# Splitting the row maxima of the windowed attention into two operations of two heads, each with its own signal

## The chip, the core and the metric

The kernel runs on one core of a Trainium2 chip, in one launch. The time is the device time of one execution in microseconds (us). Five engines work side by side and are tied together by semaphores only: TensorE (PE; its weight loads are listed as PEld), VectorE (DVE), ScalarE (ACT), GpSimd (POOL) and SyncE (SP), which issues the DMAs.

## What is computed

The reference adds four layers to `x` (16 sequences of 512 tokens, 128 features): an attention with a Gaussian kernel, a feed-forward layer, a state-space layer, and the same feed-forward layer again. The feed-forward layer has a light branch (windowed attention over all tokens) and a heavy branch (attention over routed tokens). The change is in the light branch:

```
x: (16, 512, 128); H = 8 heads of 64; windows of W = 64 tokens
q, k, v = split(layernorm(x) @ Wqkv.T, 3)
sim  = q_window . k_(previous, own, next window) / 8        # 64 x 192 for a window and head
attn = softmax(sim, axis=-1)                                # max, exp, sum, divide
o    = attn . v_(previous, own, next window)
light = o @ Wout.T
route: 50 rounds of a = logk - logsumexp(s + b), b = -relu(s + a)
```

## The kernel before, in words

The program runs `stage_rbf`, then a light stage and a heavy stage (names with `f1`), the state-space stage, and a second light and heavy stage (`f2`). The change touches `stage_light` alone, which runs twice (f1 from about 465 to 980 us, f2 from about 1206 to 1714 us).

In a light stage a **unit** is a block of 128 tokens (two windows) with four of the eight heads (`HU` = 4). A sequence has 8 units, the stage 128. A **step** t does the two units of one block of 128 tokens; there are 64 steps, four to a sequence (i = t mod 4). For a unit n the engines do this in turn:

- TensorE, `scores(n)` (L917, L903): q times k for four heads, 192 columns a head, into `sm`, which has two PSUM banks for each unit, two heads in each.
- VectorE, `maxima(n)` (L1221): one reduction of 128x768 to the 4 negated maxima `nb`.
- ScalarE, `exps(n)` (L1103): for each head exp(score - maximum) into `p`, with the row sum, which appears in the trace as an ACTIVATE and an ACTIVATION_READ_ACCUMULATOR.
- VectorE, `reciprocals(n)` (L1228); GpSimd, `normalise(n)` (L1534): `p` times the reciprocal, into `pn`.
- TensorE, `turn(n)` (L933 for the first 512 columns into `tp`, L941 for the others): transposes.
- VectorE, `leave_turned(n)` (L1234, L1236): copies them to `pt`.
- TensorE, `values(n)` (L964, L975): times v, into `xa`; ScalarE, `leave_late(n)` (L1095): copies half of it to `late`; VectorE, `leave_values(n)` (L1244): adds both halves into `ot`; TensorE, `output` (L989): times the output weights.

The order on each engine is written by hand in its function `step(t)`. Work of several steps is interleaved; the next sequence's projections go along (`use` on TensorE, L869 to L879, three a step; `leave` on ScalarE, L1077 to L1081), and so do the routing rounds (`route`, `route_shift`, `route_step`):

- TensorE: turn(2t), output, turn(2t+1), three projections, values(2t), scores(2t+4), scores(2t+5), values(2t+1). The second projection goes to `tp` and waits until the copy L1234 of unit 2t+1 has emptied it; turn(2t+1) waits for the copy L1234 of unit 2t for the same reason.
- VectorE: maxima(2t+2), maxima(2t+3), copies of unit 2t, reciprocals(2t+2), copies of unit 2t+1, residual, leave_values(2t-1), route_shift, reciprocals(2t+3), leave_values(2t).
- ScalarE: exps(2t+2) head 0, leave_late(2t-1), exps(2t+2) heads 1 to 3, exps(2t+3) heads 0 to 2, leave, exps(2t+3) head 3, leave, leave, leave_late(2t), route.

Of the kernel before, what the change touches and what calls it, by code (L numbers as in the profile page):

```python
# [10 lines left out]
ALU = mybir.AluOpType  # L11
ACT = mybir.ActivationFunctionType
AX = mybir.AxisListType.X
# [72 lines left out]
def wait(e, sem, v):  # L86

    if isinstance(v, int) and v <= 0:
        return
    e.wait_ge(sem, v)  # L90
# [601 lines left out]
def stage_light(nc, K, tag, C=None):  # L692
# [13 lines left out]
    with ExitStack() as ctx:  # L706
# [3 lines left out]
        PW = P + W  # L710
# [7 lines left out]
        nb = sb("nb", [P, 2, HU])  # L718
        sums = sb("sums", [P, 2, HU])
        rs = sb("rs", [P, 2, HU])  # L720
        p = sb("p", [P, 2, HU, PW])
# [6 lines left out]
        sm = ps("sm", [P, 2, 2, BANK])  # L728
# [17 lines left out]
        s_nb = sem("nb")  # L746
        s_ex = sem("ex")
        s_rs = sem("rs")
        s_nm = sem("nm")
# [51 lines left out]
        def place(n):  # L801

            return n // UNITS, n // UNITS % 2, n % UNITS
# [266 lines left out]
        def _(act):  # L1070
# [25 lines left out]

            def exps(n, heads):
                u = n % UNITS
                if heads[0] == 0:
                    act.wait_ge(s_nb, n + 1)  # L1100
                    wait(act, s_nm, n - 1)
                for k in heads:
                    ins = nc.scalar.activation(p[:, u % 2, k, :], sm[:, u % 2, k // 2, k % 2 * PW:(k % 2 + 1) * PW],  # L1103
                                               ACT.Exp, bias=nb[:, u % 2, k:k + 1], accum_out=sums[:, u % 2, k:k + 1])
                if heads[-1] == HU - 1:
                    ins.then_inc(s_ex, 1)
# [48 lines left out]
            if C:  # L1155
                leave_rows(0)
                leave_rows(1)
                for b in range(2, B):
                    if b < 6:
                        exps(b // 4, (b % 2 * 2, b % 2 * 2 + 1))  # L1160
                    leave_rows(b)
                    if b - 2 in WITH:
                        leave(0, WITH[b - 2])
                leave_x(1)
            else:
                exps(0, (0, 1, 2, 3))
                leave(0, 9)
                leave(0, 10)
                exps(1, (0, 1, 2, 3))
                leave(0, 11)  # L1170
                leave(0, 12)
                leave_x(1)
# [43 lines left out]
        def _(dve):  # L1216
            def maxima(n):
                b, par, u = place(n)
                dve.wait_ge(s_sm, n + 1)
                wait(dve, s_ex, n - 1)  # L1220
                nc.vector.tensor_reduce(nb[:, u % 2, :], sm[:, u % 2, :, 0:2 * PW].rearrange("p a (k c) -> p a k c", k=2),  # L1221
                                        AX, ALU.max, negate=True).then_inc(s_nb, 1)

            def reciprocals(n):
                b, par, u = place(n)
# [183 lines left out]
            if C:  # L1409
# [13 lines left out]
                for b in range(4, 9):  # L1423
                    rows(b)
                maxima(0)
                maxima(1)
                rows(9)
                rows(10)
# [7 lines left out]
                link(nc.vector.reciprocal(two[:, 1, :], two[:, 1, :]))  # L1436
                link(nc.vector.tensor_scalar(K["rc"][:], two[:, 1, :], float(np.sqrt(np.float32(E))), None, ALU.mult))
                maxima(2)
                maxima(3)
            else:  # L1440
# [1014 lines left out]
```

## Time and profile before

| | |
|---|---|
| median of 3 runs | 1840.35 us (1833.6, 1840.35, 1841.53) |
| profiled execution | 1834.43 us, span of its trace 1832.6 us |
| granted TensorE clock, mean of the span | 0.975 |
| PE busy | 1660.2 us (91%) |
| DVE busy | 1449.5 us (79%) |
| ACT busy | 1451.2 us (79%) |
| POOL busy | 748.7 us (41%) |

The profile is of one execution. Times are microseconds from the start of the span. A row of a timeline has the start, the duration, the engine, the line, the operation, what it writes and reads, and its shape; x2 means that two alike were merged, and the duration then runs from the start of the first to the end of the second. A bracket at the end is idle time of the engine just before, and what ended it. Short waits have no bracket. The ends of matmuls are modelled.

### The profile page before, as it was taken

What the parts mean: (1) busy time and instruction counts of PE and PEld (TensorE: products, weight loads), DVE (VectorE), ACT (ScalarE), POOL (GpSimd) and SP (SyncE); (2) the same over time, 40 slices, a digit from 0 to 9 for tenths busy, and PEclk for the clock granted to TensorE, in tenths of its full rate; (3) what the DMA queues carried; (4) which work ended last, traced back from release to release, by engine and by line L of the source; (5) the groups of instructions that cost most, each with busy time, mean ns of one, the idle gap of its engine ahead of it and who ended that gap; (6) DMA issues with size and microseconds to landing.
All of it is one profiled execution on the core that took longest, in us unless ns stands there. A gap on an engine that the chain in (4) does not pass through costs nothing. (4 is left out here: it accounts for less than half of the span.)

```text
span 1832.6 us, 68018 instructions
## 1 busy us (share of the span) xinstructions
PE 1660.2 (91%) x27513; PEld 1268.5 (69%) x27513; DVE 1449.5 (79%) x3461; ACT 1451.2 (79%) x4100; POOL 748.7 (41%) x842
## 2 busy tenths in 40 slices
PE   3888898886899999999997987879999999998797
PEld 1444444443688888888885874658888888887686
DVE  8999999998677777877896766747777777788574
ACT  4999999996788888888774656668888888876464
POOL 2010000000254555454545866435555555454595
PEclk7999999999999999999999997989999999999999
DMA  6555656561001010101012000001010101000211
GB/s 190 147 154 151 150 125 149 137 148 27 13 15 26 14 26 14 26 15 25 15 26 48 2 2 1 1 13 25 15 26 14 26 15 24 15 17 23 48 47 48
DMA packets 80040, 91.95 MB, mean 50 GB/s; under 512 B 11696, under 2 KB 67984, under 8 KB 79728
## 3 DMA queue, kind: packets, MB, share of 16 engines
q1 hardware_dynamic: 78432, 87.15, 19.0%
q8 instruction: 220, 3.60, 0.8%
q14 instruction: 92, 0.75, 0.1%
q10 hardware_dynamic: 1296, 0.44, 0.1%
HBM read 39.68 MB, written 31.10 MB: 39 GB/s over the span
## 5 line engine op out<-in xcount | busy, mean ns | idle before, releaser
L1534 POOL TENSOR_TENSOR f1l_pn<-f1l_p,f1l_rs 128x512 f32<-128x512 f32 (+1 forms) x256 | 206.3, 827 | 245.0 <-DVE f1l_rs L1228 240.0
L1534 POOL TENSOR_TENSOR f2l_pn<-f2l_p,f2l_rs 128x512 f32<-128x512 f32 (+1 forms) x256 | 206.2, 827 | 236.6 <-DVE f2l_rs L1228 236.6
L1103 ACT ACTIVATE f2l_p<-f2l_sm,f2l_nb 128x192 f32<-128x192 f32 x512 | 209.1, 434 | 41.7 <-DVE f2l_nb L1221 41.7
L1103 ACT ACTIVATE f1l_p<-f1l_sm,f1l_nb 128x192 f32<-128x192 f32 x512 | 209.3, 434 | 40.6 <-DVE f1l_nb L1221 37.3
L417 PE MATMUL r_acc<-r_pr,r_vp 128*32 128x128 f32 (+2 forms) x3584 | 191.4, 330 | 7.1 <-DVE r_pr L630 6.0
L527 ACT ACTIVATE r_pr<-r_far 128x1536 f32<-128x1536 f32 x128 | 194.3, 1518 | 3.3 <-PE r_far L401 3.0
L622 DVE SCALAR_TENSOR_TENSOR r_pr<-r_pr,k_lo,r_cap 128x512 f32<-128x512 f32 x256 | 181.1, 750 | 6.3 <-ACT r_pr L527 5.7
L630 DVE TENSOR_SCALAR r_pr<-r_pr,k_hi,k_lo 128x768 f32<-128x768 f32 x256 | 163.7, 683 | 0.0
L527 ACT ACTIVATE r_pr<-r_near 128x1024 f32<-128x1024 f32 x128 | 138.6, 1083 | 1.1 <-PE r_near L388 1.1
L1539 POOL MEMSET k_rtz<- 128x132 f32 x1 | 0.2, 207 | 329.4 <-POOLq L688 329.4
L1221 DVE TENSOR_REDUCE f2l_nb<-f2l_sm 128x4 f32<-128x768 f32 x128 | 116.2, 949 | 16.5 <-PE f2l_sm L917 16.5
L1221 DVE TENSOR_REDUCE f1l_nb<-f1l_sm 128x4 f32<-128x768 f32 x128 | 116.2, 949 | 13.4 <-PE f1l_sm L917 13.4
L417 PEld LDWEIGHTS r_acc<-r_pr,r_vp 128*32 128x32 f32 x3584 | 87.1, 110 | 46.8 <-issue 28.2
L1244 DVE TENSOR_TENSOR f2l_ot<-f2l_xa,f2l_late 128x256 f32<-128x256 f32 x128 | 53.9, 421 | 78.2 <-ACT f2l_late L1095 78.2
L1103 ACT ACTIVATION_READ_ACCUMULATOR f2l_p<-f2l_sm,f2l_nb 128x1 f32 x512 | 112.7, 220 | 0.0
L1103 ACT ACTIVATION_READ_ACCUMULATOR f1l_p<-f1l_sm,f1l_nb 128x1 f32 x512 | 112.5, 220 | 0.0
L1234 DVE COPY f1l_pt<-f1l_tp 128x512 f32<-128x512 f32 x128 | 88.1, 689 | 28.3 <-PE f1l_tp L933 25.1
L1234 DVE COPY f2l_pt<-f2l_tp 128x512 f32<-128x512 f32 x128 | 88.2, 689 | 23.4 <-PE f2l_tp L933 20.8
L1244 DVE TENSOR_TENSOR f1l_ot<-f1l_xa,f1l_late 128x256 f32<-128x256 f32 x128 | 53.9, 421 | 63.0 <-ACT f1l_late L1095 62.8
L917 PE MATMUL f2l_sm<-f2l_kt,f2l_qt 64*64 64x128 f32 (+1 forms) x3584 | 99.3, 248 | 0.4 <-ACT f2l_p L1103 0.4
L917 PE MATMUL f1l_sm<-f1l_kt,f1l_qt 64*64 64x128 f32 (+1 forms) x3584 | 99.1, 248 | 0.0
L964 PE MATMUL f1l_xa<-f1l_pt,f1l_vv 64*64 64x128 f32 x2048 | 85.1, 276 | 12.0 <-DVE k_x L1250 7.0
(525 smaller groups left out, 5090.5 us busy)
## 6 DMA issues: line engine op xcount, KB each, us to landing
rbf_rows<-r_part SPq DMA_DIRECT2D x112, 128.0 KB, 2.2
r_qs<-rbf_rows SPq DMA_DIRECT2D x60, 192.0 KB
r_ks<-rbf_rows SPq DMA_DIRECT2D x60, 192.0 KB
f1l_vs<-f1l_vv SPq DMA_DIRECT2D x64, 128.0 KB, 2.6
f2l_vs<-f2l_vv SPq DMA_DIRECT2D x64, 128.0 KB, 2.4
rbf_rows<-r_part SPq DMA_DIRECT2D x16, 384.0 KB, 3.2
rbf_rows<-r_part SPq DMA_DIRECT2D x16, 256.0 KB, 3.2
out<-k_x SPq DMA_DIRECT2D x8, 512.0 KB, 3.2
```

Of the source, the lines that this page charges most:

```text
L417: mm = nc.tensor.matmul(acc[32 * g:32 * g + 32, q0:q0 + n], vp[:, par, t, g, 32 * q:32 * q + 32], pr[:, (PAIRS * b + 2 * q + g // 2) % RIN ...
L527: nc.scalar.activation(pr[:, n % RING, :, cols], src, ACT.Exp).then_inc(done, 1)
L622: nc.vector.scalar_tensor_tensor(on, on, K["lo"][:, h:h + 1], cap[:, h, :].unsqueeze(1).broadcast_to([P, NT, P]), ALU.max, ALU.min)
L630: ins = nc.vector.tensor_scalar(off, off, hi, lo, ALU.min, ALU.max)
L917: mm = nc.tensor.matmul(sm[64 * w:64 * w + 64, u % 2, e, cc * PW + P * side:cc * PW + P * side + kn], qt[r, par, c, at:at + W], kt[r, par, ...
L964: nc.tensor.matmul(xa[64 * e:64 * e + 64, r, cc * P:(cc + 1) * P], vv[rows, par, i, cc, g, e, :], pt[rows, u % 2, k * P:(k + 1) * P], star ...
L1103: ins = nc.scalar.activation(p[:, u % 2, k, :], sm[:, u % 2, k // 2, k % 2 * PW:(k % 2 + 1) * PW], ACT.Exp, bias=nb[:, u % 2, k:k + 1], ac ...
L1221: nc.vector.tensor_reduce(nb[:, u % 2, :], sm[:, u % 2, :, 0:2 * PW].rearrange("p a (k c) -> p a k c", k=2), AX, ALU.max, negate=True).the ...
L1234: nc.vector.tensor_copy(pt[:, u % 2, 0:HU * P], tp[:]).then_inc(s_pt, 1)
L1244: nc.vector.tensor_tensor(ot[:, u // 2 % 2, 2 * g:2 * g + 2, :], xa[:, 0, 0:2 * P].rearrange("p (c q) -> p c q", q=P), late[:, u % 2, :].r ...
L1534: ins = nc.gpsimd.tensor_tensor(pn[:, u % 2, at:at + HU * w].rearrange("p (k c) -> p k c", k=HU), p[:, u % 2, :, cols], r.broadcast_to([P, ...
L1539: nc.gpsimd.memset(K["rtz"][:], 0.0).then_inc(s_rt, 1)
```

## The change

`maxima` issues two reductions instead of one, for heads 0 and 1 and for heads 2 and 3 (the two PSUM banks of a unit), and each raises the semaphore `s_nb` by one. `exps` waits before head 0 and again before head 2, each time for the reduction that covers the head.

```diff
             def exps(n, heads):
                 u = n % UNITS
-                if heads[0] == 0:
-                    act.wait_ge(s_nb, n + 1)
-                    wait(act, s_nm, n - 1)
                 for k in heads:
+                    if k % 2 == 0:
+                        act.wait_ge(s_nb, 2 * n + k // 2 + 1)
+                    if k == 0:
+                        wait(act, s_nm, n - 1)
...
-                nc.vector.tensor_reduce(nb[:, u % 2, :], sm[:, u % 2, :, 0:2 * PW].rearrange("p a (k c) -> p a k c", k=2),
-                                        AX, ALU.max, negate=True).then_inc(s_nb, 1)
+                for a in range(2):
+                    nc.vector.tensor_reduce(nb[:, u % 2, 2 * a:2 * a + 2],
+                                            sm[:, u % 2, a, 0:2 * PW].rearrange("p (k c) -> p k c", k=2),
+                                            AX, ALU.max, negate=True).then_inc(s_nb, 1)
```

VectorE, at the start of a step in f2's light stage, before (in brackets the semaphores that an instruction waits for: l_sm is signalled by the scores, l_ex by the exps, l_t4 by the transposes L933):

```order
L1244 TENSOR_TENSOR f2l_ot<-f2l_xa,f2l_late 128x256 [waits l_w,l_ov]
L1221 TENSOR_REDUCE f2l_nb<-f2l_sm 128x4 [waits l_ex,l_sm] x2
L1234 COPY f2l_pt<-f2l_tp 128x512 [waits l_t4,l_pv]
L1236 COPY f2l_pt<-f2l_pj 128x256 [waits l_t]
L1261 SCALAR_TENSOR_TENSOR k_na<-k_lns,k_m,k_router_rows 128x1 [waits l_sl]
```

The same place now (lines after the change are 3 higher):

```order
L1247 TENSOR_TENSOR f2l_ot<-f2l_xa,f2l_late 128x256 [waits l_w,l_ov]
L1223 TENSOR_REDUCE f2l_nb<-f2l_sm 128x2 [waits l_ex,l_sm]
L1223 TENSOR_REDUCE f2l_nb<-f2l_sm 128x2
L1223 TENSOR_REDUCE f2l_nb<-f2l_sm 128x2 [waits l_ex,l_sm]
L1223 TENSOR_REDUCE f2l_nb<-f2l_sm 128x2
L1237 COPY f2l_pt<-f2l_tp 128x512 [waits l_t4,l_pv]
```

Two reductions have become four; nothing else has moved. ScalarE, from the end of one step into the next, before (l_nb is the maxima's signal, l_nm GpSimd's, l_pv that of the values, l_pp that of a projection):

```order
L1131 ACTIVATE k_lns<-k_sum 128x1 [waits l_sl]
L1103 ACTIVATE f2l_p,f2l_sums<-f2l_sm,f2l_nb 128x192 [waits l_nm,l_nb]
L1095 ACTIVATE f2l_late<-f2l_xa 128x256 [waits l_oe,l_pv]
L1103 ACTIVATE f2l_p,f2l_sums<-f2l_sm,f2l_nb 128x192 x3
L1103 ACTIVATE f2l_p,f2l_sums<-f2l_sm,f2l_nb 128x192 [waits l_nm,l_nb]
```

The same place now:

```order
L1132 ACTIVATE k_lns<-k_sum 128x1 [waits l_sl]
L1104 ACTIVATE f2l_p,f2l_sums<-f2l_sm,f2l_nb 128x192 [waits l_nm,l_nb]
L1095 ACTIVATE f2l_late<-f2l_xa 128x256 [waits l_oe,l_pv]
L1104 ACTIVATE f2l_p,f2l_sums<-f2l_sm,f2l_nb 128x192
L1104 ACTIVATE f2l_p,f2l_sums<-f2l_sm,f2l_nb 128x192 [waits l_nb]
L1104 ACTIVATE f2l_p,f2l_sums<-f2l_sm,f2l_nb 128x192
L1104 ACTIVATE f2l_p,f2l_sums<-f2l_sm,f2l_nb 128x192 [waits l_nm,l_nb]
```

The order is the same; each unit's third head has a wait that it had not.

## Rows read from the trace of the kernel before

**Rows 1.** Busy time of each engine in the two light stages.
```profile
core 0: us, PE busy (x) PEld busy (x) DVE busy (x) ACT busy (x) POOL busy (x), PEclk, DMA share, GB/s
465.00:980.00 515.00, 498.44 (x9364) 421.39 (x9362) 403.07 (x1054) 425.85 (x1526) 254.01 (x306) 1.00 0.08 19
1206.00:1714.00 508.00, 491.85 (x9344) 420.50 (x9344) 378.29 (x909) 416.54 (x1508) 254.08 (x306) 1.00 0.08 19
```
**Rows 2.** The instructions and waits around the tile nb, f1's and f2's.
```profile
L1221 DVE TENSOR_REDUCE f1l_nb<-f1l_sm x128: 947/948/958, 470.1 to 968.4; 128x4 f32<-128x768 f32 x128
  ACT f1l_p L1103: 37.3, 58
...
L1221 DVE TENSOR_REDUCE f2l_nb<-f2l_sm x128: 947/948/959, 1214.6 to 1696.0; 128x4 f32<-128x768 f32 x128
...
  ACT f2l_p L1103: 41.7, 63
```
**Rows 3.** Timeline of VectorE, from a step with i = 1 into that with i = 3.
```profile
1380.01 1.81 DVE L1221 TENSOR_REDUCE f2l_nb<-f2l_sm 128x4 f32<-128x768 f32 x2
1381.77 0.69 DVE L1234 COPY f2l_pt<-f2l_tp 128x512 f32<-128x512 f32 x1
...
1383.35 0.69 DVE L1234 COPY f2l_pt<-f2l_tp 128x512 f32<-128x512 f32 x1 [0.15 <-PE f2l_tp L933]
...
1387.06 0.42 DVE L1244 TENSOR_TENSOR f2l_ot<-f2l_xa,f2l_late 128x256 f32<-128x256 f32 x1 [1.43 <-ACT f2l_late L1095]
1387.40 1.81 DVE L1221 TENSOR_REDUCE f2l_nb<-f2l_sm 128x4 f32<-128x768 f32 x2
1389.32 0.69 DVE L1234 COPY f2l_pt<-f2l_tp 128x512 f32<-128x512 f32 x1
...
1395.63 1.82 DVE L1221 TENSOR_REDUCE f2l_nb<-f2l_sm 128x4 f32<-128x768 f32 x2 [0.60 <-PE f2l_sm L917]
1397.61 0.69 DVE L1234 COPY f2l_pt<-f2l_tp 128x512 f32<-128x512 f32 x1 [0.16 <-PE f2l_tp L933]
```
**Rows 4.** Timeline of TensorE over the same time.
```profile
1380.85 0.23 PE L975 MATMUL f2l_xa<-f2l_pt,f2l_vs 64*64 64x64 f32 x2
1381.01 0.66 PE L933 MATMUL f2l_tp<-k_ident,f2l_pn 128*128 128x128 f32 x4
...
1382.61 0.63 PE L933 MATMUL f2l_tp<-k_ident,f2l_pn 128*128 128x128 f32 x4
...
1384.09 0.50 PE L869 MATMUL f2l_tp<-f_xh,k_wqkv_l 128*128 128x512 f32 x1
...
1385.68 0.67 PE L964 MATMUL f2l_xa<-f2l_pt,f2l_vv 64*64 64x128 f32 x16
...
1388.56 0.66 PE L933 MATMUL f2l_tp<-k_ident,f2l_pn 128*128 128x128 f32 x4
...
1390.16 0.62 PE L933 MATMUL f2l_tp<-k_ident,f2l_pn 128*128 128x128 f32 x4
...
1396.84 0.66 PE L933 MATMUL f2l_tp<-k_ident,f2l_pn 128*128 128x128 f32 x4
```
**Rows 5.** Timeline of ScalarE, the step with i = 1.
```profile
1380.28 0.20 ACT L1131 ACTIVATE k_lns<-k_sum 128x1 f32<-128x1 f32 x1
1380.99 0.42 ACT L1103 ACTIVATE f2l_p<-f2l_sm,f2l_nb 128x192 f32<-128x192 f32 x1 [0.51 <-DVE f2l_nb L1221]
...
1381.40 0.37 ACT L1095 ACTIVATE f2l_late<-f2l_xa 128x256 f32<-128x256 f32 x1
...
1385.79 0.60 ACT L1079 ACTIVATE f2l_kt<-f2l_pj 128x512 f32<-128x512 f32 x1
1386.65 0.38 ACT L1095 ACTIVATE f2l_late<-f2l_xa 128x256 f32<-128x256 f32 x1 [0.26 <-PE f2l_xa L975]
```
**Rows 6.** Reductions of another width, in the heavy stage (by line and shape; mean in ns).
```profile
L1927 DVE TENSOR_REDUCE f2h_nb<-f2h_ps 128x4 f32<-128x516 f32 x16 | 10.4, 690 | 19.6 <-PE f2h_ps L1725 19.6
```
**Rows 7.** Timeline of VectorE at the start of f2's light stage.
```profile
1217.32 0.18 DVE L1228 RECIPROCAL f2l_rs<-f2l_sums 128x4 f32<-128x4 f32 x1 [0.92 <-ACT f2l_p L1103]
1219.90 0.18 DVE L1228 RECIPROCAL f2l_rs<-f2l_sums 128x4 f32<-128x4 f32 x1 [2.40 <-ACT f2l_p L1103]
```

## The prediction

> **What bounds the kernel now.** I read the busy times by stage first [rows 1]. In both light stages TensorE is busy for 97% of the time at the full granted clock, VectorE for 74 to 78%, ScalarE for 82 to 83%, GpSimd for half. No engine is plainly full but TensorE, whose ends are modelled, so the limit has to be read from the waits. Next the tile that the change splits: ScalarE waited 37.3 us in 58 waits (f1) and 41.7 us in 63 waits (f2) for the maxima [rows 2]. That is 79 us of waiting, and the question is whether any of it is on the path. So third, the timelines of one sequence's steps, where the period of a step is 7.39 us (1380.01 to 1387.40) or 8.23 us (1387.40 to 1395.63) [rows 3].
>
> Followed back, the loop is this. VectorE copies the transposed unit 2t out of `tp` (starts 1381.77, ends 1382.46) [rows 3]; TensorE's next transposes start at 1382.61, a hand-over later, and end at 1383.24 [rows 4]; VectorE copies again at 1383.35 with a wait marked for just these [rows 3], ending at 1384.04; TensorE's second projection, which needs that bank, starts at 1384.09, the values at 1385.68 [rows 4]; ScalarE takes them out at 1386.65, having idled 0.26 us for TensorE [rows 5]; VectorE adds them at 1387.06, having idled 1.43 us, and then comes to the next two maxima at 1387.40 [rows 3]. The maxima stand on this loop where the copy behind them is late because of them. The exps do not: between the first exp and the late copy at 1386.65 ScalarE twice had to wait for TensorE's products anyway.
>
> **Is the copy behind the maxima late because of them?** Two readings of the same instant. By TensorE: the transposes of unit 2t end at 1381.67 and the copy starts at 1381.77, 0.10 later; the transposes that end at 1383.24 are followed by a copy at 1383.35, 0.11 later and marked as a wait [rows 3, 4]. So the copy started when TensorE let it. By VectorE: two reductions take 1.81 us together and one takes 0.948 [rows 2, 3], so the second starts 0.86 after the first and 0.09 before the record of the first ends; the copy could thus have started at 1380.01 + 1.81 - 0.08 = 1381.74. VectorE was ready 0.03 us before TensorE. This is the tight kind of step, i = 0 and 1. In the step with i = 2 VectorE was ready at 1387.40 + 1.73 = 1389.13 and the copy started at 1389.32 (transposes end 1389.22): 0.19 us of slack. With i = 3, 1395.63 + 1.74 = 1397.37 against 1397.61: 0.24 us [rows 3, 4]. These are the loose kind. The four steps repeat in the other sequences of both stages.
>
> **The change part by part.**
>
> *One more reduction for each unit, 256 in all.* A reduction of 768 elements takes 0.948 us [rows 2], one of 516 takes 0.690 [rows 6]: 1.02 ns an element. One of 384 comes to 0.948 - 0.39 = 0.56 us. From start to start it takes 0.08 to 0.09 less, as the pairs show, so about 0.47, and the two halves 0.94 instead of 0.86 to 0.87: 0.07 us more for each unit, 0.14 for each step. The bounds: at least 0.06 (what is left if the element takes a little more), and at most the whole fixed part of a record, 0.948 - 768 x 0.00102 = 0.16 us, if two halves do not overlap as two wholes do. I take 0.07, because the pairs of [rows 3] already have a signal and a wait between them and overlap all the same.
>
> *In a tight step* 0.14 us, less 0.03 of slack, goes on the loop: 0.11. There are 64 such steps in two stages; the first of each stage, and the ones where TensorE is late by more (around the start and the end of the routing search), do not count, so I take 60: 60 x 0.11 = 6.6 us.
>
> *In a loose step* 0.14 us disappears under the 0.19 or 0.24 us that the copy waits for TensorE. Cost 0. That cover is gone above 0.19.
>
> *ScalarE's first exp starts earlier.* It started at 1380.99, 0.03 us behind the first reduction's end (1380.96), after 0.51 us of idling [rows 3, 5]. With half the reduction it can start 0.39 us earlier. But the next instruction there is the late copy of unit 2t-1, which needs the values whose matmuls end at 1381.08 [rows 4] and started at 1381.40 [rows 5] only because the exp was in front of it; it can move up 0.26 at most with its hand-over. So the exps behind it gain some 0.26 us. What waits for them: the reciprocals, which are ahead of GpSimd's work, which has a whole step to spare; the late copy of unit 2t, which waits for TensorE already (0.26 idle). Worth 0 on the loop. What is late next is TensorE, as before.
>
> *The added wait, before head 2.* Its signal comes 0.47 us after the first one's, while head 0, the late copy and head 1 take over 0.9 us of ScalarE. So it is never waited for; the wait itself is issued on an engine with slack ahead of the late copy. Cost 0, at worst a few hundredths that the 0.26 covers.
>
> *The start of a stage* is a plain chain: there VectorE waited 0.92 and 2.40 us for the exps [rows 7], and the first maxima are in front of them. Up to 0.39 us is gained in each stage: -0.8 us.
>
> *Sum:* 6.6 - 0.8 = +5.8 us on the profiled execution's 1834.43, that is 1840.2. The median shown is 5.9 us above that execution; what I compare with is the median, so 1840.35 + 5.8 = 1846 us.
>
> The Trainium skill, in "VectorE: DVE Perf Modes", section "The DRAIN you can't avoid", says that the next operation does not start before the pipeline has emptied; its section on the errata puts the fixed term of an operation at about 150 cycles, 0.156 us, and its rules for authors say to minimise the count of operations. The trace shows the overlap of 0.09 us between two reductions, so I read the price of one more as 0.07; by the page's term it would be an estimate of 0.156, which is the first rival's price.
>
> **The rivals.**
>
> *1. The full fixed part is paid.* If each half costs 0.16 us more, a step costs 0.32. Tight steps: 0.29 x 60 = 17 us; loose steps: 0.13 and 0.08, 30 of each: 6 us. With the starts, +22.6, so 1863 us. For it: no row shows two reductions of the same unit without a wait between, nor one of 384 elements. Against: every pair of rows of VectorE that stands back to back overlaps.
>
> *2. ScalarE sets the end (faster).* If the loop is really closed by ScalarE, from first exp to late copy, then every one of the 121 waits [rows 2] shortens by 0.26 us (the late copy of unit 2t-1 holds the rest back): -31 us, 1809. For it: the 79 us of waits, and only 0.26 us of idling ahead of the late copy. It decides as soon as that 0.26 is not a true wait. Against: the bracket names TensorE's L975 as what ended it [rows 5], and in the same step VectorE and TensorE hand over to each other without a gap.
>
> *3. Nothing is on the path.* If the slack of a tight step is more than the 0.03 read, say TensorE's transposes have 0.1 to give before the next transposes are late, the reductions cost nothing anywhere and the two starts gain: 1839 to 1841 us. For it: TensorE is 97% busy and may itself be the limit. Against: the second transposes start 0.15 behind the end of the copy in the tight step (1382.46, 1382.61) and in the loose one (1390.01, 1390.16) [rows 3, 4]; a queue of TensorE's own would not keep that distance when the copy moves.
>
> **How the numbers follow.** My forecast (+3 to +9 us) has 0.55, rival 1 (or a price between) 0.17, rival 2 or a part of it 0.12, rival 3 0.16. About 0.5%, 9.2 us, is what a measurement can tell from no change. Faster by more than that is rival 2 alone: 0.12. Slower by more is rival 1 and the upper end of my own: 0.23. The rest, 0.65, is the same. The forecast's own range is 1843 to 1850; for 8 in 10 it reaches up to rival 1's time and down past rival 3 some way into the partial gains: 1830 to 1863.
>
> **What would show it.** Right: reductions of about 0.56 us, four of them in 1.88 to 1.96 us from the first start to the last end; the copy L1234 behind them 1.87 us after the first start in tight steps (before 1.76), its distance to the transposes larger than 0.10 there and unchanged in loose ones; a tight step's period up by 0.1, the loose ones' unchanged; ScalarE's wait ahead of the first exp down from 0.51 to about 0.1, and a new wait ahead of the late copy that follows it. Wrong: tight periods that are unchanged (rival 3), loose periods longer (rival 1), or the late copy of unit 2t earlier relative to the maxima in every step (rival 2).

## The result and the profile after

The changed kernel takes 1842.33 us (median of 20 runs, 1836.08 to 1848.83), the kernel before 1839.61 us in the runs beside it (20 runs, 1833.6 to 1844.07). The ratio is 1.0023, with an interval of 1.0013 to 1.0033: 4.2 us slower, 2.4 to 6.1 (the two medians alone differ by 2.7 us, the two means by 3.8). That is a real difference, and within 0.5%. The profiled execution took 1842.14 us, its span is 1840.4 us, the granted clock 0.971 over the span (0.975 before). In the bulk of both light stages (500 to 960 us and 1240 to 1690 us) the clock is 1.00 in both traces, so what the steps there take is compared at one clock. VectorE has 256 instructions more and is busy for 1458.6 us instead of 1449.5.

The reductions first, by tile, with those who waited for them (min/median/max in ns, first and last start; this answers to [rows 2]):

```profile
L1223 DVE TENSOR_REDUCE f1l_nb<-f1l_sm x256: 543/547/558, 471.8 to 972.4; 128x2 f32<-128x384 f32 x128
...
  ACT f1l_p L1104: 14.7, 13
```
```profile
L1223 DVE TENSOR_REDUCE f2l_nb<-f2l_sm x256: 543/547/558, 1219.9 to 1704.0; 128x2 f32<-128x384 f32 x128
...
  ACT f2l_p L1104: 14.8, 15
```

A half takes 0.547 us, and ScalarE's listed waits for the maxima have fallen from 79.0 us in 121 waits to 29.5 us in 28, while the kernel became slower. The list overstates what went. It leaves out short waits, and the usual wait is now such a short one, of 0.11 us; counted in full from the traces, ScalarE's idling ahead of a unit's first exp falls from 82.3 to 37.3 us. Most of that went elsewhere: all idle time of ScalarE in the two light stages, every gap counted, is 171.0 us now and was 176.6.

VectorE in three steps, of the kinds that [rows 3] shows: 1378.08 and 1385.45 begin tight steps, 1392.94 and 1401.16 loose ones.

```profile
1378.08 1.94 DVE L1223 TENSOR_REDUCE f2l_nb<-f2l_sm 128x2 f32<-128x384 f32 x4
1379.94 0.68 DVE L1237 COPY f2l_pt<-f2l_tp 128x512 f32<-128x512 f32 x1
...
1385.45 1.94 DVE L1223 TENSOR_REDUCE f2l_nb<-f2l_sm 128x2 f32<-128x384 f32 x4
1387.31 0.68 DVE L1237 COPY f2l_pt<-f2l_tp 128x512 f32<-128x512 f32 x1
1388.87 0.69 DVE L1237 COPY f2l_pt<-f2l_tp 128x512 f32<-128x512 f32 x1 [0.34 <-PE f2l_tp L933]
1392.60 0.42 DVE L1247 TENSOR_TENSOR f2l_ot<-f2l_xa,f2l_late 128x256 f32<-128x256 f32 x1 [1.44 <-ACT f2l_late L1095]
1392.94 1.94 DVE L1223 TENSOR_REDUCE f2l_nb<-f2l_sm 128x2 f32<-128x384 f32 x4
1394.86 0.69 DVE L1237 COPY f2l_pt<-f2l_tp 128x512 f32<-128x512 f32 x1
...
1401.16 1.95 DVE L1223 TENSOR_REDUCE f2l_nb<-f2l_sm 128x2 f32<-128x384 f32 x4 [0.59 <-PE f2l_sm L917]
1403.14 0.69 DVE L1237 COPY f2l_pt<-f2l_tp 128x512 f32<-128x512 f32 x1
```

Four halves take 1.94 us from first start to last end, where two wholes took 1.81. In a tight step the copy starts 1.86 us behind the first of them (1385.45 to 1387.31); before it was 1.76 (1380.01 to 1381.77 in [rows 3]). In a loose step it is 1.92 and 1.98, as before. The medians over the steps of each kind say the same. They are given for i = 0, 1, 2, 3, worked out from the starts in the two traces; the period is that from one step's first maxima to the next step's:

| from the first maxima of a step to | before | after |
|---|---|---|
| the copy behind them | 1.76, 1.76, 1.92, 1.98 | 1.86, 1.86, 1.92, 1.98 |
| the first exp | 0.98, 0.98, 0.98, 0.99 | 0.58, 0.58, 0.58, 0.65 |
| the late copy of unit 2t-1 | 1.39, 1.39, 1.39, 1.40 | 1.14, 1.14, 1.28, 1.34 |
| the late copy of unit 2t (f1) | 6.52, 6.63, 6.79, 6.74 | 6.61, 6.73, 6.79, 6.73 |
| period (f1) | 7.28, 7.39, 8.23, 7.49 | 7.37, 7.49, 8.23, 7.49 |
| all four steps of a sequence, the sum of these | 30.39 | 30.57 |

The row on the late copy of unit 2t tells how far ScalarE's head start reaches: it has the first exp 0.40 us earlier and, in tight steps, the first late copy 0.26 earlier, but the late copy at the end of the step, which the loop goes through, is 0.09 to 0.10 later where the copy was delayed and unchanged elsewhere. ScalarE in the step that begins at 1385.45 shows where the gained time went (compare [rows 5]):

```profile
1385.72 0.20 ACT L1132 ACTIVATE k_lns<-k_sum 128x1 f32<-128x1 f32 x1
1386.03 0.42 ACT L1104 ACTIVATE f2l_p<-f2l_sm,f2l_nb 128x192 f32<-128x192 f32 x1
...
1386.59 0.39 ACT L1095 ACTIVATE f2l_late<-f2l_xa 128x256 f32<-128x256 f32 x1
...
1389.71 0.60 ACT L1079 ACTIVATE f2l_kt<-f2l_xa 128x512 f32<-128x512 f32 x1 [0.33 <-PE f2l_xa L873]
...
1392.18 0.38 ACT L1095 ACTIVATE f2l_late<-f2l_xa 128x256 f32<-128x256 f32 x1 [0.26 <-PE f2l_xa L975]
```

The 0.51 us of idling ahead of the first exp is down to 0.11 (1385.92 to 1386.03). The late copy that follows starts 0.56 us behind the exp instead of 0.41: a short new wait for the values. Six exps later ScalarE comes 0.33 us too early for a projection, and ahead of the late copy of unit 2t it idles 0.26 us, just as before.

The stages, from the first maxima to the last `ot`, are 516.84 and 499.51 us long, against 513.59 and 497.07: +3.3 and +2.4. That is 5.7 of the 7.8 us between the two spans; the other 2 us lie outside the light stages, where nothing was changed. The runs of either kernel lie 10 to 13 us apart, so 2 us between two executions need no cause of their own.

### The profile page after: what moved, and what is told of

Read it like the earlier page. It is cut to its first block and busy times, and to the rows that moved or that the text cites. A ratio compares the mean times of both kernels' runs of the same rounds, so it can differ in the third digit from the quotient of the medians.

```text
span 1840.4 us, 68274 instructions
## 1 busy us (share of the span) xinstructions
PE 1669.7 (91%) x27513; PEld 1273.7 (69%) x27513; DVE 1458.6 (79%) x3717; ACT 1463.2 (80%) x4100; POOL 749.3 (41%) x842
## 5 line engine op out<-in xcount | busy, mean ns | idle before, releaser
L1104 ACT ACTIVATE f2l_p<-f2l_sm,f2l_nb 128x192 f32<-128x192 f32 x512 | 209.0, 430 | 18.8 <-DVE f2l_nb L1223 14.8
L1223 DVE TENSOR_REDUCE f2l_nb<-f2l_sm 128x2 f32<-128x384 f32 x256 | 124.3, 547 | 16.2 <-PE f2l_sm L917 16.2
L1223 DVE TENSOR_REDUCE f1l_nb<-f1l_sm 128x2 f32<-128x384 f32 x256 | 124.4, 547 | 13.6 <-PE f1l_sm L917 13.6
L1237 DVE COPY f1l_pt<-f1l_tp 128x512 f32<-128x512 f32 x128 | 87.7, 685 | 27.7 <-PE f1l_tp L933 27.3
L1237 DVE COPY f2l_pt<-f2l_tp 128x512 f32<-128x512 f32 x128 | 87.7, 685 | 23.3 <-PE f2l_tp L933 22.4
```

The lines of the kernel that those rows point to most:

```text
L1223: nc.vector.tensor_reduce(nb[:, u % 2, 2 * a:2 * a + 2], sm[:, u % 2, a, 0:2 * PW].rearrange("p (k c) -> p k c", k=2), AX, ALU.max, negate ...
L1237: nc.vector.tensor_copy(pt[:, u % 2, 0:HU * P], tp[:]).then_inc(s_pt, 1)
```

## The experiments

Each was timed side by side with the kernel before, in 4 to 12 executions, and the ratios are to that kernel. The edits of 1 to 4, 7 and 9 are shown against the changed kernel, those of 5, 6 and 8 against the kernel before. L numbers are those of each kernel's own lines. "A sequence takes" stands for the sum of the four periods, as in the table above; in f1 and f2 of one trace it agrees within 0.03 us.

**1. Two reductions, but ScalarE waits for both.** It separates the cost on VectorE from the gain on ScalarE.

```diff
-                    if k % 2 == 0:
-                        act.wait_ge(s_nb, 2 * n + k // 2 + 1)
                     if k == 0:
+                        act.wait_ge(s_nb, 2 * n + 2)
```

> The two reductions of each unit stay, but ScalarE waits for both of them before head 0, as before the change. Theory (the cost is VectorE's added time on the loop through the copies, and ScalarE's earlier start buys nothing but the start of each stage): the same time as the changed kernel within 1.5 us, ratio to before 1.002 to 1.004; tight steps at 7.36 and 7.48 us as in the changed kernel. Rival (the early start was worth something all along and paid a part of a larger cost): slower than the changed kernel by what it was worth, up to 0.26 us in each of some 120 steps, 31 us; ratio above 1.006.

Measured: 1843.75 us, ratio 1.0025 (1.0013 to 1.0037). ScalarE waits again, more than before the change:

```profile
L1222 DVE TENSOR_REDUCE f2l_nb<-f2l_sm x256: 544/548/559, 1220.6 to 1706.3; 128x2 f32<-128x384 f32 x128
...
  ACT f2l_p L1103: 46.3, 63
```

14.8 us of waits have become 46.3 (41.7 before the change), and the four steps of a sequence take the same 30.57 us as with the early start. In steady state the second signal is worth nothing. The light stages are 0.85 and 1.4 us longer than in the changed kernel. Only part of this lies at a start: in f2 the first copy L1237 (here L1236) starts 7.74 us behind the stage's first maxima, against 7.29 in the changed kernel, and in f1 there is no difference. The rest comes in a few jumps of 0.3 to 1.1 us at single steps later in the stages; such jumps also lie between the other traces, and their cause was not looked for.

**2 and 3. The halves in loose steps only, and in tight steps only.** The same edit with opposite sets, (2, 3) in experiment 2 and (0, 1) in 3; the counts of the semaphore follow it.

```diff
+        def halved(n):
+            return (n // 2 - 1) % NT in (2, 3)
+
+        def signals(n):
+            return sum(1 + halved(m) for m in range(n))
...
+                    if k == 0 or (k == 2 and halved(n)):
+                        act.wait_ge(s_nb, signals(n) + k // 2 + 1)
...
+                if halved(n):
...
+                else:
+                    nc.vector.tensor_reduce(nb[:, u % 2, :],
...
```

> Units whose maxima are taken in steps with i = 2 or 3 are halved, the others have one reduction as before the change. Theory: the copy behind them waits 0.19 to 0.24 us for TensorE there, which covers 0.13 us: ratio to before 0.999 to 1.001, periods of all four steps as before (7.27, 7.39, 8.22, 7.49). Rival (each added reduction costs its time wherever it stands): half of the change's cost, +2 to +3 us, ratio 1.001 to 1.0015, with the periods behind i = 2 and 3 longer by 0.1.

> Units whose maxima are taken in steps with i = 0 or 1 are halved, the others have one reduction. Theory: the whole cost of the change, +4 to +6 us, ratio 1.002 to 1.003, tight periods longer by 0.09, the others as before. Rival (cost wherever it stands): half of it, ratio 1.001 to 1.0015.

Measured: loose only 1837.53 us, ratio 0.9995 (0.998 to 1.0009); tight only 1842.71 us, ratio 1.0022 (1.0009 to 1.0035). So the 64 tight steps, of 128 in the two stages, carry the loss: with them alone it is there, with the loose ones alone none is measured. VectorE with halves in loose steps (first a tight step, then a loose one):

```profile
1377.91 1.81 DVE L1234 TENSOR_REDUCE f2l_nb<-f2l_sm 128x4 f32<-128x768 f32 x2
1379.67 0.69 DVE L1248 COPY f2l_pt<-f2l_tp 128x512 f32<-128x512 f32 x1
...
1393.86 1.95 DVE L1230 TENSOR_REDUCE f2l_nb<-f2l_sm 128x2 f32<-128x384 f32 x4 [0.59 <-PE f2l_sm L923]
1395.84 0.69 DVE L1248 COPY f2l_pt<-f2l_tp 128x512 f32<-128x512 f32 x1
```

And with halves in tight steps:

```profile
1379.80 1.94 DVE L1230 TENSOR_REDUCE f2l_nb<-f2l_sm 128x2 f32<-128x384 f32 x4
1381.66 0.68 DVE L1248 COPY f2l_pt<-f2l_tp 128x512 f32<-128x512 f32 x1
...
1403.23 1.82 DVE L1234 TENSOR_REDUCE f2l_nb<-f2l_sm 128x4 f32<-128x768 f32 x2 [0.60 <-PE f2l_sm L923]
1405.21 0.69 DVE L1248 COPY f2l_pt<-f2l_tp 128x512 f32<-128x512 f32 x1 [0.16 <-PE f2l_tp L939]
```

The distance from maxima to copy is 1.76 (tight, whole), 1.98 (loose, halved), 1.86 (tight, halved) and 1.98 (loose, whole). A loose step has the same length with either, apart from the bracket: with halves VectorE's idling ahead of the copy, 0.16 us for TensorE, is nearly used up. A sequence takes 30.40 us with halves in loose steps and 30.57 with halves in tight ones.

**4. Four reductions for each unit, one for each head.** This goes past the slack of every step.

```diff
-                for a in range(2):
-                    nc.vector.tensor_reduce(nb[:, u % 2, 2 * a:2 * a + 2],
...
+                for k in range(HU):
+                    nc.vector.tensor_reduce(nb[:, u % 2, k:k + 1], sm[:, u % 2, k // 2, k % 2 * PW:(k % 2 + 1) * PW],
+                                            AX, ALU.max, negate=True).then_inc(s_nb, 1)
...
+                    if k % 2 == 0:
-                        act.wait_ge(s_nb, 2 * n + k // 2 + 1)
+                        act.wait_ge(s_nb, 4 * n + k + 2)
```

> Four reductions for each unit, of one head each; ScalarE waits for two of them before head 0 and for all before head 2. A step has 6 more reductions than before the change, at 0.065 us from start to start: +0.39 us on VectorE. Theory (VectorE's time counts above each step's slack of 0.03, 0.03, 0.19 and 0.24 us): 0.36 in 60 tight steps, 0.20 and 0.15 in 30 loose steps each, 21.6 + 6 + 4.5 = 32 us less about 0.5 at the starts; ratio 1.015 to 1.019. Rival (proportional to the number of reductions, 4.2 us for two more in each step): 12.6 us, ratio 1.007. Rival (the cost lies in signals and waits, not in VectorE's time): ScalarE has no more waits than in the changed kernel, so 1.002 to 1.004.

Measured: 1868.75 us, ratio 1.0155 (1.0131 to 1.0179), some 28 us. The reductions and copies, a tight step and a loose one:

```profile
L1223 DVE TENSOR_REDUCE f2l_nb<-f2l_sm x512: 344/348/359, 1232.9 to 1730.5; 128x1 f32<-128x192 f32 x171
```
```profile
1379.10 2.20 DVE L1223 TENSOR_REDUCE f2l_nb<-f2l_sm 128x1 f32<-128x192 f32 x8
1381.22 0.68 DVE L1236 COPY f2l_pt<-f2l_tp 128x512 f32<-128x512 f32 x1
...
1387.51 2.21 DVE L1223 TENSOR_REDUCE f2l_nb<-f2l_sm 128x1 f32<-128x192 f32 x8 [0.59 <-PE f2l_sm L917]
1389.63 0.68 DVE L1236 COPY f2l_pt<-f2l_tp 128x512 f32<-128x512 f32 x1
```

The copy now starts 2.12 us behind the first maxima in every step, tight or loose (2.13 with i = 3): VectorE sets it everywhere. Six more reductions in a step take 2.20 - 1.81 = 0.39 us more, 0.065 each. A sequence takes 31.40 us, 1.01 more than before. By the copies, unrounded, the tight steps pay 0.35 each and the loose ones 0.20 and 0.15, 1.05 together.

**5. One reduction over two heads, for all four.** It leaves out the maxima of heads 2 and 3: one 128x384 reduction for heads 0 and 1, whose two maxima serve heads 2 and 3 as well.

```diff
-                                               ACT.Exp, bias=nb[:, u % 2, k:k + 1], accum_out=sums[:, u % 2, k:k + 1])
+                                               ACT.Exp, bias=nb[:, u % 2, k % 2:k % 2 + 1], accum_out=sums[:, u % 2, k:k + 1])
...
-                nc.vector.tensor_reduce(nb[:, u % 2, :], sm[:, u % 2, :, 0:2 * PW].rearrange("p a (k c) -> p a k c", k=2),
+                nc.vector.tensor_reduce(nb[:, u % 2, 0:2],
+                                        sm[:, u % 2, 0, 0:2 * PW].rearrange("p (k c) -> p k c", k=2),
```

> One reduction for each unit, over heads 0 and 1 only, and heads 2 and 3 use those two maxima as their own (part of the maxima is left out): VectorE has 0.40 us less for each unit, 0.80 less for each step, and ScalarE can start 0.4 us earlier, more than any split could give. Theory (with the maxima out of the way TensorE's own chain sets the loop): only the slack that VectorE lacked and the starts are gained, 0 to 0.03 us a step; ratio 0.996 to 1.000. Rival (VectorE or ScalarE sets the loop and the change would have paid with a cheaper reduction): 0.26 to 0.8 us a step, 30 to 90 us, ratio 0.95 to 0.985.

Measured: 1836.56 us, ratio 0.9986 (0.9973 to 1.0000). VectorE in a tight step:

```profile
1379.37 1.14 DVE L1221 TENSOR_REDUCE f2l_nb<-f2l_sm 128x2 f32<-128x384 f32 x2
1381.14 0.69 DVE L1235 COPY f2l_pt<-f2l_tp 128x512 f32<-128x512 f32 x1 [0.62 <-PE f2l_tp L933]
```

VectorE is ready 0.67 us sooner (1.14 instead of 1.81) and waits 0.62 us for TensorE's transposes; the copy still starts 1.76 us behind the maxima (median), and a sequence takes 30.41 us. So before the change TensorE, not VectorE, let the copy start, and there is nothing to win on VectorE's side of this place. The 3 us of the median are not in the steps of the trace, and its interval touches 1. The expectation counted on 0.80 us less for VectorE. The missing part is the overlap: these two reductions, of different units, start 0.58 us apart or more in all but three pairs, at least 0.03 behind the end of the record in front, where halves of the same width in the changed kernel start 0.464 apart. Why they don't overlap here stays open.

**6 and 7. The transposes of the next unit ahead of the values.** If TensorE's transposes are what the copy waits for, having them earlier should speed up the kernel and bring the price of the halves back in all steps. On TensorE `turn(2t+2)` moves from the start of a step to ahead of `values(2t+1)` of the step before; experiment 6 does it to the kernel before, 7 to the changed one.

```diff
-                turn(2 * t)
+                if t == 0:
+                    turn(0)
...
+                if t + 1 < T:
+                    turn(2 * t + 2)
                 values(2 * t + 1)
```

> The kernel before, with one move on TensorE: the transposes of unit 2t+2 are issued ahead of the values of unit 2t+1 instead of behind them, so that the copy behind the maxima waits for VectorE alone and starts 1.73 us after the first maxima in every step (1.76, 1.76, 1.92 and 1.98 us before). Theory A (the copy's start is what a step turns on, as in the prediction): the loop is shorter by 0.03, 0.03, 0.19 and 0.25 us, 0.5 a sequence, 15 us in two stages; ratio 0.991 to 0.994. Theory B (TensorE's own work between the two transposes, the values and the output, is only just covered by that copy, and is now moved between them): the second transposes start when they did, the gain is under 0.03 us a step; ratio 0.998 to 1.001.

> The changed kernel with the same move on TensorE. Theory A: the copy starts 1.86 us after the first maxima in every step, against 1.76, 1.76, 1.92 and 1.98 us before: -0.10, -0.10, +0.06, +0.12 us a sequence of gain, so about the time of the kernel before, ratio 0.999 to 1.002. Theory B: the tight steps stay 0.09 us longer than before and the loose ones do not gain: the changed kernel's time, ratio 1.001 to 1.004. In either case the split costs against e6, since with TensorE out of the way VectorE's added 0.13 us stands uncovered in all four steps: by 0.10 to 0.13 us a step, 12 to 16 us, under A, and by 5 to 8 us under B.

Measured: 1881.63 us, ratio 1.0244 (1.0224 to 1.0264), and 1882.8 us, ratio 1.0249 (1.0225 to 1.0273). Both expectations missed by far. ScalarE and VectorE in a tight step of experiment 6:

```profile
1405.94 0.42 ACT L1106 ACTIVATE f2l_p<-f2l_sm,f2l_nb 128x192 f32<-128x192 f32 x1 [0.51 <-DVE f2l_nb L1224]
...
1407.06 0.38 ACT L1098 ACTIVATE f2l_late<-f2l_xa 128x256 f32<-128x256 f32 x1 [0.61 <-PE f2l_xa L975]
```
```profile
1404.96 1.81 DVE L1224 TENSOR_REDUCE f2l_nb<-f2l_sm 128x4 f32<-128x768 f32 x2
1406.69 0.68 DVE L1237 COPY f2l_pt<-f2l_tp 128x512 f32<-128x512 f32 x1
...
1408.68 0.18 DVE L1231 RECIPROCAL f2l_rs<-f2l_sums 128x4 f32<-128x4 f32 x1 [0.86 <-ACT f2l_p L1106]
1408.78 0.67 DVE L1237 COPY f2l_pt<-f2l_tp 128x512 f32<-128x512 f32 x1
```

The copy did start earlier: 1.73 us behind the maxima in every step (1.74 with i = 3), as VectorE alone allows. Against the 1.76, 1.76, 1.92 and 1.98 of before, this measures the slack that the prediction had read: 0.03, 0.03, 0.19 and 0.24 us. But the values behind the transposes are later, and ScalarE's late copy of unit 2t-1 waits for them *in front of* the exps of heads 1 to 3: 2.10 us behind the maxima instead of 1.39. The exps are late, the reciprocals wait for them, and the second copy stands behind the reciprocals on VectorE: 2.09 us after the first (1406.69 to 1408.78) instead of 1.57. A sequence takes 32.22 us. Experiment 7, where the copy stands 1.86 us behind the maxima, takes the same 32.22. The loop had changed its course, so the pair says little on what the earlier transposes are worth.

**8 and 9. The same, with the late copy behind three exps.** To take that block away: on ScalarE `exps(2t+2)` of heads 0 to 2, then `leave_late(2t-1)`, then head 3. Experiment 8 is 6 with this edit, 9 is 7 with it.

```diff
-                    exps(2 * t + 2, (0,))
+                    exps(2 * t + 2, (0, 1, 2))
...
-                    exps(2 * t + 2, (1, 2, 3))
+                    exps(2 * t + 2, (3,))
```

> As e6 (transposes of unit 2t+2 ahead of the values of unit 2t+1), and ScalarE takes the late copy of unit 2t-1 behind heads 0 to 2 of the next unit instead of behind head 0. In e6 that late copy waited 0.6 us for TensorE and held back the exps, so that VectorE's reciprocals (39.9 us in 42 waits) and the copy behind them came late. Theory (that hold-up was all of e6's loss): the reciprocals wait no longer, and the question of e6 can be answered: gain of the copy's start by 0.03, 0.03, 0.19 and 0.25 us passed on (A, ratio 0.991 to 0.994) or kept by TensorE's own work between the two transposes (B, 0.998 to 1.002). Rival (the values behind the transposes make everything after them late as well, the adds and the output): still over 1.015.

> e8 with the maxima in two halves. Under A: slower than e8 by 0.13 us in each step, 12 to 16 us, as nothing covers VectorE's time; under B: slower than e8 by 3 to 8 us. Rival: if exps are what VectorE waits for in e8, the earlier first exp is worth something at last, up to 0.4 us a step, and e9 is faster than e8.

Measured: 1864.79 us, ratio 1.0149 (1.0132 to 1.0167), and 1867.17 us, ratio 1.0164 (1.0147 to 1.0181). The block is gone (VectorE's waits for exps ahead of the reciprocals, from 1250 to 1600 us, are 4.9 us where experiment 6 had 39.9), and 17 us came back. Neither theory that was put down for 8 came true (ratio 0.991 to 0.994, or 0.998 to 1.002); its rival, that the later values make what follows late as well, asked for over 1.015 and is the nearest. For 9 at least 3 us over 8 were expected; the medians differ by 2.4 us, with intervals that overlap. VectorE in experiment 9:

```profile
1403.96 1.94 DVE L1226 TENSOR_REDUCE f2l_nb<-f2l_sm 128x2 f32<-128x384 f32 x4
1405.82 0.68 DVE L1240 COPY f2l_pt<-f2l_tp 128x512 f32<-128x512 f32 x1
1407.63 0.69 DVE L1240 COPY f2l_pt<-f2l_tp 128x512 f32<-128x512 f32 x1 [0.57 <-PE f2l_tp L933]
```

The first copy is 1.86 behind the maxima, as in the changed kernel, but the second waits 0.57 us for TensorE, and a sequence takes 31.70 us with whole reductions and with halves. Here the halves are hidden in every step, tight or not. What keeps these two slow is, by this, TensorE's own sequence. TensorE in experiment 8:

```profile
1403.19 1.52 PE L917 MATMUL f2l_sm<-f2l_kt,f2l_qt 64*64 64x128 f32 x64
1404.64 0.66 PE L933 MATMUL f2l_tp<-k_ident,f2l_pn 128*128 128x128 f32 x4
1405.13 0.38 PE L941 MATMUL f2l_pj<-k_ident,f2l_pn 128*128 128x128 f32 x2
1405.44 0.67 PE L964 MATMUL f2l_xa<-f2l_pt,f2l_vv 64*64 64x128 f32 x16
...
1406.15 1.16 PE L989 MATMUL f2l_xa<-k_wout_l,f2l_ot 128*128 128x128 f32 x8
1407.15 0.60 PE L933 MATMUL f2l_tp<-k_ident,f2l_pn 128*128 128x128 f32 x4
```

and in the kernel before (its rows from the first transposes on are in [rows 4]):

```profile
1379.01 1.52 PE L917 MATMUL f2l_sm<-f2l_kt,f2l_qt 64*64 64x128 f32 x64
1380.35 0.62 PE L964 MATMUL f2l_xa<-f2l_pt,f2l_vv 64*64 64x128 f32 x16
```

From the scores to the second transposes it is 3.96 us (1403.19 to 1407.15) against 3.60 (1379.01 to 1382.61) for the same work, and there the second transposes stand 0.15 us behind the end of a copy that they wait for, so TensorE's own part is 3.60 at most. Four times 0.36 is 1.4 us a sequence, and 1.3 were lost (31.70 against 30.39). The order 64x64 tiles, 128x128, 64x64, 128x128 has two changes more than 64x64, then 128x128. That the changes themselves cost the 0.36 us is read from this order and was not tried alone.

## Why the prediction was right, point by point

1846 us was forecast with an own range of 1843 to 1850 and a wider one of 1830 to 1863; 1842.33 was measured, which is in the wider range and 0.7 us below the own one. The forecast as a difference was +5.8 us (+3 to +9), the measured one +4.2 (2.4 to 6.1). The call "within 0.5%" held. Of the 3.7 us between 1846 and 1842.33, 0.7 are the base: 1840.35 was the median of three runs, 1839.61 that of twenty.

- *What bounds the kernel.* Right. The loop goes over the copy, TensorE and the late copy; giving ScalarE all of its waits for the maxima back cost nothing in steady state (experiment 1), and halving VectorE's maxima left the copy where it was (experiment 5).
- *The price of one more reduction, taken as 0.07 of 0.06 to 0.16.* Measured 0.065, and the same by two halves as by four quarters. The records are 0.948, 0.547 and 0.348 us for 768, 384 and 192 elements, 1.04 ns an element and a fixed part of 0.148; two of them back to back overlap by about 0.083, and the rest is 0.065. The price was the difference of two nearly equal numbers, the fixed part and the overlap, and both could be read from the kernel before.
- *Tight steps, 0.11 each.* Right in kind, a little high: 0.09 to 0.10. The copy came 0.096 later; behind four halves it also takes 0.68 instead of 0.69 us. The price was taken 0.005 too high for each reduction, and the slack of 0.03 was right. By the periods that is 0.18 us a sequence (0.09 and 0.10 in tight steps, nothing in loose ones), and over all 32 sequences of both stages 32 x 0.18 = 5.8 us against the 6.6 forecast.
- *Loose steps, 0.* Right: 1.92 and 1.98 unchanged, and experiment 2 measured 0.9995 (0.998 to 1.0009). Experiment 4 shows the cover's end: with 0.39 us more the loose steps pay too. The slack can be priced from one trace: it is what the release by the other engine leaves over.
- *The earlier exp.* Right: the late copy of unit 2t-1 moved by 0.26 in tight steps, as forecast, the other 0.15 became the new wait ahead of it, and its 0.26 ended in a wait for a projection.
- *The starts of the stages, -0.8 us.* Half right: -0.4 us, in f2 alone. From the stage's first maxima to its first copy out of `tp` f2 takes 7.68 us before and 7.29 after. It is also 7.29 in experiments 2 and 5, where the first reduction is short and signals at once, and 7.74 in 1, where ScalarE waits for both. In f1 it is 22.66 before and 22.69 after: there VectorE waits 6.19 us for TensorE ahead of that copy, and an earlier exp gains nothing. The prediction carried over to f1 a wait that it had read in f2 alone [rows 7].
- *The added wait, 0.* Right: ScalarE has no gap at all ahead of a third head, in either stage.

With the start as measured the sum is 5.8 - 0.4 = 5.4 us, and the stages are 5.7 us longer in the one pair of traces.

Rival 1 (1863 us) fell: the records show the fixed part, but in the changed kernel the overlap stays, between the two halves of a unit as between two units. (Its own terms, 17.4 + 6.3 - 0.8, come to +22.9, not +22.6.) The Trainium skill, "VectorE: DVE Perf Modes", in "The DRAIN you can't avoid", qualifies its own rule: a next operation that isn't held, that is, needn't let all earlier ones finish, starts earlier. The trace agrees, by 0.083 us for each of these; the full fixed part of 0.148 would have cost more than twice what was paid. Rival 2 (1809 us) fell: the waits ahead of the first exp did shrink, and no period did. Rival 3 fell: it needed more than 0.03 us of slack in tight steps, and experiment 3 shows the loss there. Its picture, TensorE as the limit, holds in the loose steps and, as far as experiments 8 and 9 show, in the kernels with reordered transposes.

No version tried is faster than the kernel before by more than the noise. Experiment 5 comes nearest (0.9986, up to 1.0000), and it leaves out half of the maxima.

## What to carry to other kernels

Before splitting an operation to signal earlier, follow what the waiting engine does next: a wait that ends sooner is worth only what moves up at the next hand-over on the loop. Here that was nothing, against a price of 0.065 us for each operation added. A list of waits that has become shorter is no sign of a gain by itself; look whether the engine's idle time as a whole has, and the period. Whether the price is paid differs from step to step of the same loop, and can be read beforehand: compare the time at which the busy engine was ready with the time at which the other engine released the operation behind. A steady distance from the other engine's end, in steps of both kinds, is the sign of who releases it.

## What the runs showed of the hardware

- A 128x192, 128x384 and 128x768 maximum reduction out of PSUM take 0.348, 0.547 and 0.948 us in the records; back to back, in the kernel before, the changed one and experiment 4, each starts 0.083 us before the record in front of it ends. In experiment 5 nearly all pairs of 128x384 do not overlap and start 0.58 us apart or more.
- A 128x512 copy out of PSUM takes 0.66 to 0.68 us where it starts 0.08 to 0.09 us before the record in front of it ends, and 0.69 everywhere else.
- The same TensorE work took 3.96 us instead of at most 3.60 with transposes (128x128 tiles) set between two groups of 64x64 tiles.
- On ScalarE a single copy that waits for TensorE cost 17 us by standing ahead of two exps instead of behind them (experiments 6 and 8), once it started 0.7 us later than before.
